# A graph network kernel: packed window lengths and running pair numbers kept in registers while the edge counts are made

## The chip, the cores and the metric

The program runs on one core of one Trainium2 chip. The metric is device time in microseconds (us) for one execution, lower is better. Before the change three executions took 4158.90, 4162.92 and 4170.17 us, so the median is 4162.92 us. All rows below come from one further execution that the hardware profiler took.

## The reference

Four graph layers run over N = 3125 nodes with 128 features and E = 100000 edges, given as `src` and `dst` with `dst` sorted. Each layer is followed by `x = layernorm(x + layer(x))`.

- Layer 0: an MLP over `concat(x[src], x[dst])` for each edge, two linear maps with batch norm and relu, summed over the edges of each `dst`.
- Layer 1: two graph convolutions with self loops and the norm `dinv[src] * dinv[dst]`, one along the edges and one against them.
- Layer 2: four steps `h = h + relu(tanh(A_norm @ (h @ Weff.T) - relu(h @ Asym.T)))`.
- Layer 3: attention with 8 heads over the edges, softmax over the edges of each target.

Layers 1 to 3, and the batch norm statistics of layer 0, need the edges only as a matrix of counts: `C[d, s]` is the number of edges from node s to node d. The kernel makes this matrix once and the change lies in that stage. `dst` is drawn as `3125 * u**2`, so low nodes have many edges and high nodes few.

## The kernel before, in words

Features are padded to NP = 3200 nodes. Every engine has its own program, and engines meet by semaphores only (`S[...]`). The stages are: preparation; the counts stage; degrees and batch norm statistics, which read the counts back; "pass 1" over the edges (layer 0, first map); "pass 2"; the graph convolutions; the four steps; attention.

The counts stage makes 100 windows (NWIN) of 32 targets each. The source axis is cut in four parts of 800, so a window is a 128 x 800 matrix in two PSUM banks: row 4*(target - 32*w) + (part of the source), column = source within its part. Edges come in pairs of 128-edge tiles: 392 pairs (NPAIR) of 256 edges. A window w visits the pairs `first` to `end - 1` that hold its targets, at least two. A pair on the border of two windows is visited by both. For each visit:

- VectorE (`one_hots`) builds for two tiles the one-hot rows of the sources (`one_src`, two 128 x 800 instructions, line 1392) and of the targets (`one_dst`, one 128 x 256 instruction, line 1394) in one of 8 slots (PAIRS). It waits for `slot_free` and tells `one_ready`.
- TensorE (`count_pair`) waits for `one_ready`, does four matmuls (two tiles, two halves of 400 columns, line 1746) into the banks `w mod 3` (SETS), and tells `slot_free`.

The slot and both semaphore values are worked out from a running number: `before + p` counts all visits so far from PAIR0 = 512 on, so `before` of a window is (visits done) - `first`. The function `window` (lines 388 to 397) gets these on each engine. It reads one packed word of the window from SBUF (`block_tab` row 3, `end * 512 + first`, line 390, a TENSOR_LOAD), takes it apart (lines 391 and 392), and either reads `before` from row 2 of the table (line 394, for the first window of a Python group) or works it out from the window ahead of it (line 396). Each value passes a range check, which is some register instructions and a SEQ_ASSERT.

TensorE's order in a window (`count_group`, lines 1767 to 1786; 12 windows are written out in a group and a hardware loop runs over the groups): `window`; wait until the low part of window w - 3 is out of the same banks (`lo_made`); the first pair; `low_part(w-2)`, which takes the bf16 part off what is in PSUM (line 1766); `source_degrees(w-3)` (line 1757); a hardware loop over the pairs that are left (line 1783); and a matmul with zeros that tells `window_done` (line 1785). VectorE's order (`count_four`, lines 1400 to 1408; four windows are written out): `window`, the first pair, and a hardware loop over the others (line 1407).

ScalarE (`evict`, `store_low`) handles each window in four passes: row counts and the bf16 part (lines 964 and 965), the f32 counts (line 966), the low part (line 976), a square that finds counts beyond bf16 (line 982). It issues three DMAs (lines 969, 970, 980). GpSimd gathers rows of `a_table` for pass 1 (line 817, 24 gathers in a round of six groups). It is told when it may go on: in the rounds 1 to 13 by `one_ready` at least 28 further visits on in each round, in the rounds 14 to 16 by `window_done`, at the last one 92 windows; after that it runs free. SP stores what was gathered (line 605). TensorE's fourth unit of pass 1 reads the first rows that GpSimd gathers straight into `a_direct`, after all 22 rounds.

The tables come from the preparation, on VectorE: `visits(block_tab, NWIN, PAIR0)` (line 1359) and one instruction that packs row 3 (line 1360). A helper on each engine, `do`, waits for each of these instructions before the next one.

Of the kernel before, what the change touches and what calls it, by code (L numbers as in the profile page):

```python
# [101 lines left out]
def gnn(nc, ins, out):  # L102
# [26 lines left out]
    with ctx:  # L129
# [54 lines left out]
        block_tab = sb("block_tab", [1, 4, NWIN], i32)  # L184
# [50 lines left out]
        lim_i = sb("lim_i", [NWIN, 2], i32)  # L235

# [94 lines left out]
        def bank(j, n=BANK):  # L331
            return psum[:, j * BANK:j * BANK + n]
# [55 lines left out]
        def window(eng, w, done_pairs):  # L388

            word = eng.value_load(block_tab[0:1, 3, ds(w, 1)], min_val=0, max_val=NPAIR * 512 + NPAIR)  # L390
            first = nc.s_assert_within(eng.snap(word & 511), 0, NPAIR - 2)
            end = nc.s_assert_within(eng.snap(word >> 9), 2, NPAIR)
            if done_pairs is None:
                before = eng.value_load(block_tab[0:1, 2, ds(w, 1)], min_val=PAIR0 - NPAIR, max_val=PAIR0 + NWIN * NPAIR)
            else:
                before = nc.s_assert_within(eng.snap((done_pairs - first) & 65535), PAIR0 - NPAIR, PAIR0 + NWIN * NPAIR)
            return first, end, before
# [858 lines left out]
        def _(dve):  # L1256
            v = nc.vector

            def do(i):
                stepped("dve", dve, i)  # L1260
# [98 lines left out]
            visits(block_tab, NWIN, PAIR0)  # L1359
            do(v.scalar_tensor_tensor(block_tab[:, 3, :], block_tab[:, 1, :], 512.0, block_tab[:, 0, :], ALU.mult, ALU.add))  # L1360
# [38 lines left out]

            def count_four(i):  # L1400
                done_pairs = None
                for q in range(4):
                    w = 4 * i + q
                    first, end, before = window(dve, w, done_pairs)
                    done_pairs = before + end
                    one_hots(w, first, before)
                    with dve.Fori(first + 1, end) as p:
                        one_hots(w, p, before)

# [310 lines left out]
        def _(pe):  # L1720
# [48 lines left out]

            def count_group(g, ms):  # L1770
                done_pairs = None
                for m in ms:
                    w = GROUP * g + m
                    known = isinstance(w, int)
                    first, end, before = window(pe, w, done_pairs)
                    done_pairs = before + end
                    after(pe, S["lo_made"], w + -2)
                    count_pair(m % SETS, first, before, True)
# [4 lines left out]
                    with pe.Fori(first + 1, end) as p:  # L1783
                        count_pair(m % SETS, p, before, False)
# [442 lines left out]
```

How the kernel before makes its waits and increments, by code:

```python
        def after(eng, s, n):  # L368
            if not (isinstance(n, int) and n <= 0):
                eng.wait_ge(s, n)
# [1 line left out]
        def hold(name, eng, s, n):  # L373
            eng.wait_ge(s, n)
            eng.sem_inc(held[name], 1)
# [42 lines left out]
        def stepped(name, eng, i):  # L419
            steps[name] += 1
            i.then_inc(step[name], 1)
            eng.wait_ge(step[name], steps[name])
# [13 lines left out]
        def stage_start(name, eng):  # L437
            passed[name] += 1
            for e in done:
                eng.wait_ge(done[e], passed[name])
# [47 lines left out]
        def root_act(act, to, of, bias):  # L489
            n = roots["act"] = roots["act"] + 1
            act.wait_ge(S["root_asked"], n)
            nc.scalar.activation(to, of, ACT.Sqrt, bias=bias).then_inc(S["root_made"], 1)
# [1 line left out]
        def root_dve(dve, to):  # L495
            n = roots["dve"] = roots["dve"] + 1
            dve.sem_inc(S["root_asked"], 1)
            dve.wait_ge(S["root_made"], n)
            stepped("dve", dve, nc.vector.reciprocal(to, to))
# [7 lines left out]
        def norm_pe(pe):  # L508
# [5 lines left out]
            def variances(c):  # L514
                pe.wait_ge(S["ln_sq"], squared + c + 1)
                for b in blocks_of(c):
                    last = nc.tensor.matmul(bank(7)[:, b:b + 1], z[:, b * P:(b + 1) * P], meanf[:, 0:1],
                                            start=True, stop=True)
                return last
# [7 lines left out]
            variances(NCH - 2)  # L527
            variances(NCH - 1).then_inc(S["ln_psum"], 1)
            pe.wait_ge(S["ln_dve"], given + 2 * NCH + 1)
            for c in range(NCH):
```

## Time and profile before

| what | value |
|---|---|
| median of three executions | 4162.92 us |
| profiled execution, its own time | 4158.93 us |
| its span, first to last instruction | 4157.3 us |
| TensorE busy in the span | 3405.6 us (82%) |
| VectorE busy | 2768.4 us (67%) |
| ScalarE busy | 1590.5 us (38%) |
| GpSimd busy | 1047.6 us (25%) |
| mean granted TensorE clock | 0.936 of full speed |

The profiled execution's own time is 1.6 us above its span and 4 us below the median. The counts stage runs from about 80 to 841 us, 18% of the span.
### The profile page before, as it was taken

To read this page: it belongs to the slowest core of one execution; us is meant where nothing else is said; L and a number is where in the kernel's file an instruction comes from. 1 tells how busy PE (TensorE), PEld (TensorE's weight loads), DVE (VectorE), ACT (ScalarE), POOL (GpSimd) and SP (SyncE) were. 2 spreads that over 40 slices of the span, in tenths; PEclk is the share of its full clock that TensorE was granted. 3 is DMA by queue.
4 is the path that set the end of the run, shared out by engine and by line. 5 is a ranking of instruction groups with operands and counts; after the bars stand their busy time and mean duration, and the time that the engine had idled before them with its cause. 6 is when DMAs were issued, how large, how long until landed. Compare 5 with 4: busy or idle time off the path is not lost. (4 is left out here: it accounts for less than half of the span.)

```text
span 4157.3 us, 85411 instructions
## 1 busy us (share of the span) xinstructions
PE 3405.6 (82%) x20244; PEld 1671.3 (40%) x20359; DVE 2768.4 (67%) x3753; ACT 1590.5 (38%) x2188; POOL 1047.6 (25%) x1132
## 2 busy tenths in 40 slices
PE   3777777777889967777989996699799989989996
PEld 1333333333444456666545554233322233332223
DVE  6887766623666655565122215799799989989995
ACT  2134455521222245543102111221198841118883
POOL 2877774566666312221000001000100000000000
PEclk8989899878999999999999998899899999999998
DMA  2245665667777667676646774411154431103343
GB/s 61 91 163 192 211 223 193 213 224 244 251 250 236 210 222 212 204 205 192 237 158 222 252 254 118 120 55 55 38 144 121 131 96 55 58 25 128 110 131 69
DMA packets 359411, 662.48 MB, mean 159 GB/s; under 512 B 134549, under 2 KB 221715, under 8 KB 358545
## 3 DMA queue, kind: packets, MB, share of 16 engines
q1 hardware_dynamic: 236288, 360.99, 27.4%
q10 hardware_dynamic: 97940, 248.84, 17.5%
q0 software_dynamic: 25088, 51.43, 4.7%
q8 instruction: 54, 0.88, 0.1%
q14 instruction: 41, 0.34, 0.0%
HBM read 428.22 MB, written 208.17 MB: 153 GB/s over the span
## 5 line engine op out<-in xcount | busy, mean ns | idle before, releaser
L817 POOL DMA_INDIRECT gat<-a_table,gidx x592 | 678.6, 1146 | 240.1 <-issue 138.4
L1697 DVE SCALAR_TENSOR_TENSOR pw<-ex,c_full 128x1564 f32<-128x1564 f32 x400 | 680.8, 1780 | 35.3 <-ACT ex L1235 30.7
L1235 ACT ACTIVATE ex<-psum 128x782 f32<-128x782 f32 x800 | 610.3, 826 | 77.2 <-PE psum L2117 61.0
L1659 DVE CUSTOM_DVE_ANT_0 masked<-psum,masks 128x1784 bf16<-128x1784 f32 x320 | 552.3, 1784 | 64.5 <-ACT masks L1208 43.4
L1746 PE MATMUL psum<-one_src,one_dst 128*128 x1968 | 420.2, 354 | 204.4 <-DVE one_dst L1394 117.4
L1392 DVE TENSOR_SCALAR one_src<-iota_sub,src_low 128x800 f16 x984 | 381.7, 429 | 196.8 <-PE psum L1746 115.0
L2126 PE MATMUL psum<-pw,vaug 128*32 128x391 f32 x3200 | 348.7, 508 | 29.8 <-DVE pw L1697 9.4
L1746 PEld LDWEIGHTS psum<-one_src,one_dst 128*128 x1968 | 189.7, 101 | 419.7 <-issue 336.0
L1208 ACT ACTIVATE masks<-masks,far 128x3128 bf16<-128x3128 bf16 x40 | 115.5, 2900 | 424.8 <-DMA masks<-ct_parts 424.8
L1058 ACT ACTIVATE r<-psum,vec 128x1024 f32<-128x1024 f32 x98 | 118.1, 1205 | 368.4 <-PE psum L1897 365.0
L1533 DVE SCALAR_TENSOR_TENSOR u<-psum,u 128x1024 f16<-128x1024 f32 x98 | 120.0, 1224 | 200.3 <-ACT u L1109 200.2
L1945 PE MATMUL psum<-w2s,r_in 128*128 128x128 f32 x1568 | 209.3, 289 | 35.8 <-issue 24.3
L1394 DVE SCALAR_TENSOR_TENSOR one_dst<-row_c,window_at,iota_row 128x256 f16 x492 | 233.9, 475 | 0.0
L2082 PE MATMUL psum<-qp,kp 96*128 96x446 bf16 (+1 forms) x700 | 173.0, 364 | 61.3 <-DVE mx L1659 31.8
L817 POOL DMA_INDIRECT a_direct<-a_table,gidx x192 | 184.3, 960 | 118.4 <-DMA a_direct<-a_table,gidx 58.7
L899 POOL TENSOR_TENSOR y<-y,visit_sum 128x128 f32 x122 | 102.3, 839 | 438.8 <-ACT visit_sum L1120 438.8
L1958 PE MATMUL psum<-u,ohd 128*128 128x128 f16 x1952 | 144.9, 226 | 82.8 <-issue 45.6
L1945 PEld LDWEIGHTS psum<-w2s,r_in 128*128 128x128 f32 x1568 | 191.2, 199 | 51.6 <-issue 43.8
L1499 DVE CAST dst_bc<-psum 128x1024 f16<-128x1024 f32 x98 | 120.0, 1225 | 114.7 <-PE psum L1897 109.8
L2087 PE MATMUL psum<-qp,kp 96*128 96x448 bf16 x800 | 189.6, 360 | 0.0
L1904 PE MATMUL psum<-r,W2T 128*128 128x512 f32 x392 | 184.3, 592 | 0.0
L2117 PE MATMUL psum<-kp,qp 99*128 (+1 forms) x800 | 173.0, 337 | 13.6 <-ACTq L1217 7.9
(350 smaller groups left out, 4842.9 us busy)
## 6 DMA issues: line engine op xcount, KB each, us to landing
c_full<-c_whole SPq DMA_DIRECT2D x80, 977.5 KB, 5.1
r_edges<-r ACTq DMA_DIRECT2D x98, 512.0 KB
r_in<-r_edges ACTq DMA_DIRECT2D x98, 512.0 KB, 3.9
c_ring<-ct_parts SPq DMA_DIRECT2D x100, 480.0 KB, 4.4
c_whole<-c_sum ACTq DMA_DIRECT2D x100, 400.0 KB
a_edges<-gat SPq DMA_DIRECT2D x148, 256.0 KB
a_in<-a_edges ACTq DMA_DIRECT2D x74, 512.0 KB, 4.3
c_ring<-ct_parts SPq DMA_DIRECT2D x100, 320.0 KB, 3.6
```

Source lines behind the costliest of these rows:

```text
L817: g.indirect_dma_start(to, None, a_table, bass.IndirectOffsetOnAxis(ap=gidx[:, s, k:k + 1], axis=0)).then_inc(landed, 16)
L1235: a.activation(ex[:, step_slot(n // 2), (n % 2) * 2 * CW:(n % 2 + 1) * 2 * CW].rearrange("p (h t) -> p h t", h=2), psum[:, o:o + 2 * BANK] ...
L1392: v.tensor_scalar(one_src[:, ds(slot, 1), t, 0:SUB].rearrange("p o n -> p (o n)"), iota_sub[:, :], src_low[:, ds(p * 2 + t, 1)], None, ALU ...
L1394: v.scalar_tensor_tensor(one_dst[:, ds(slot, 1), :, :].rearrange("p o t n -> p (o t) n"), row_c[:, ds(p * 2, 2)].rearrange("p (t o) -> p t ...
L1659: v.tensor_tensor_reduce(out=masked[:, n % 2, 0:count * width].rearrange("p (c t) -> p c t", c=count), in0=psum[:, first * BANK:(first + c ...
L1697: v.scalar_tensor_tensor(pw[:, step_slot(k), :].rearrange("p (h t) -> p h t", h=HQ), ex[:, step_slot(k), :].rearrange("p (h t) -> p h t", ...
L1746: last = t.matmul(bank(2 * k + half, n), one_dst[:, ds(slot, 1), s, :].rearrange("p o n -> p (o n)"), one_src[:, ds(slot, 1), s, half * HA ...
L1904: last = t.matmul(bank(4 + 2 * s + half), W["W2T"][:, :], r1[:, s, half * GE:(half + 1) * GE], start=True, stop=True)
L1945: last = t.matmul(psum[:, s * UE + k * P:s * UE + (k + 1) * P], r1_in[:, s, k * P:(k + 1) * P], w2s[:, :], start=False, stop=True, skip_gr ...
L2082: last = t.matmul(bank(first + c, width), kp[0:KQK, n // 2, ds(b * P, P)], query(quad, n // 2)[0:KQK, c0 + c * width:c0 + (c + 1) * width] ...
L2087: t.matmul(bank(7, 448), kp[0:KQK, n // 2, 0:P], query(quad, n // 2)[0:KQK, 0:448], start=True, stop=True)
L2126: last = t.matmul(psum[hh * HW:(hh + 1) * HW, 6 * BANK:6 * BANK + CW], vaug[:, k, quad * HQ + hh, :], pw[:, step_slot(k), hh * CW:(hh + 1) ...
```

## The change

TensorE no longer reads a word for each window. A new table `length_tab` has one word for three windows (SETS), with 9 bits for each window's number of pairs; TensorE reads it for each third window and takes the length by shift and mask. It no longer needs `first` (its slots and semaphore values need the running number only), so its loop runs over 1 to length - 1. The running number stays in a register, `pairs_taken`, that is copied into `before` with a range check and raised at the window's end. VectorE still needs `first`, to find the edges; it reads the packed words of four windows by one call ahead of the four windows, and keeps its own running number in a register. In the preparation, `visits(block_tab, ...)` (five instructions) goes, and six instructions that make `length_tab` come.

```diff
-        def window(eng, w, done_pairs):
-            word = eng.value_load(block_tab[0:1, 3, ds(w, 1)], min_val=0, max_val=NPAIR * 512 + NPAIR)
-            first = nc.s_assert_within(eng.snap(word & 511), 0, NPAIR - 2)
-            end = nc.s_assert_within(eng.snap(word >> 9), 2, NPAIR)
-            if done_pairs is None:
-                before = eng.value_load(block_tab[0:1, 2, ds(w, 1)], min_val=PAIR0 - NPAIR, max_val=PAIR0 + NWIN * NPAIR)
-            else:
-                before = nc.s_assert_within(eng.snap((done_pairs - first) & 65535), PAIR0 - NPAIR, PAIR0 + NWIN * NPAIR)
-            return first, end, before
+        def pairs_before(eng, total):
+            return nc.s_assert_within(eng.snap(total), PAIR0, PAIR0 + NWIN * NPAIR)
...
-            visits(block_tab, NWIN, PAIR0)
-            do(v.scalar_tensor_tensor(block_tab[:, 3, :], block_tab[:, 1, :], 512.0, block_tab[:, 0, :], ALU.mult, ALU.add))
+            do(v.scalar_tensor_tensor(block_tab[:, 2, :], block_tab[:, 1, :], 512.0, block_tab[:, 0, :], ALU.mult, ALU.add))
+            do(v.memset(lengths[:, :, :], 0))
+            do(v.tensor_tensor(lengths[:, :, :].rearrange("p t k -> p (t k)")[:, 0:NWIN], block_tab[:, 1, :],
+                               block_tab[:, 0, :], ALU.subtract))
+            for k in range(1, SETS):
+                do(v.tensor_single_scalar(shifted[:, :, k:k + 1], lengths[:, :, k:k + 1], 9 * k, op=ALU.logical_shift_left))
+            do(v.tensor_tensor(shifted[:, :, 0:1], lengths[:, :, 0:1], shifted[:, :, 1:2], ALU.bitwise_or))
+            do(v.tensor_tensor(length_tab[:, :].rearrange("p (t o) -> p t o", o=1), shifted[:, :, 0:1], shifted[:, :, 2:3],
+                               ALU.bitwise_or))
...
+            total_dve = dve.alloc_register("pairs_made")
+            dve.reg_mov(total_dve, PAIR0)
             def count_four(i):
-                done_pairs = None
+                words = nc.values_load_multi_w_load_instructions(
+                    block_tab[0:1, 2, ds(4 * i, 4)], engines=[dve.engine], min_val=0, max_val=NPAIR * 512 + NPAIR)[1]
                 for q in range(4):
+                    first = nc.s_assert_within(dve.snap(words[q] & 511), 0, NPAIR - 2)
+                    end = nc.s_assert_within(dve.snap(words[q] >> 9), 2, NPAIR)
+                    before = nc.s_assert_within(dve.snap((pairs_before(dve, total_dve) - first) & 65535), PAIR0 - NPAIR,
+                                                PAIR0 + NWIN * NPAIR)
                     w = 4 * i + q
-                    first, end, before = window(dve, w, done_pairs)
-                    done_pairs = before + end
                     one_hots(w, first, before)
                     with dve.Fori(first + 1, end) as p:
                         one_hots(w, p, before)
+                    dve.reg_add(total_dve, total_dve, end - first)
...
+            total_pe = pe.alloc_register("pairs_taken")
+            pe.reg_mov(total_pe, PAIR0)
             def count_group(g, ms):
-                done_pairs = None
                 for m in ms:
...
-                    first, end, before = window(pe, w, done_pairs)
-                    done_pairs = before + end
+                    if m % SETS == 0:
+                        word = pe.value_load(length_tab[0:1, ds((GROUP // SETS) * g + m // SETS, 1)], min_val=0,
+                                             max_val=NPAIR << 9 * (SETS - 1) | NPAIR << 9 | NPAIR)
+                    length = nc.s_assert_within(pe.snap((word >> 9 * (m % SETS)) & 511), 2, NPAIR)
+                    before = pairs_before(pe, total_pe)
                     after(pe, S["lo_made"], w + -2)
-                    count_pair(m % SETS, first, before, True)
+                    count_pair(m % SETS, 0, before, True)
...
-                    with pe.Fori(first + 1, end) as p:
+                    with pe.Fori(1, length) as p:
                         count_pair(m % SETS, p, before, False)
+                    pe.reg_add(total_pe, total_pe, length)
```

## Rows read from the trace of the kernel before

**Rows 1.** Two stretches: us, busy (x) PE, PEld, DVE, ACT, POOL; clock, DMA, GB/s.

```profile
79.00:554.00 475.00, 348.62 (x1646) 156.95 (x1647) 373.91 (x1007) 165.27 (x290) 382.57 (x353) 0.91 0.48 161
554.00:842.00 288.00, 208.95 (x1012) 92.39 (x1010) 177.00 (x471) 166.82 (x300) 164.46 (x190) 0.90 0.61 209
```

**Rows 2.** Who waited for whom, 80 to 851: total us, times, longest.

```profile
PEld psum L1746 <- issue: 336.0, 455, 4.1
DVE one_src L1392 <- PE psum L1746: 115.0, 86, 2.4
DVE one_src L1392 <- issue: 80.8, 54, 2.6
POOL gidx L814 <- PE psum L1785: 66.3, 13, 20.9
```

**Rows 3.** Waits for a pair (whole stage, then before 554.5 us); windows closed.

```profile
L1746 PEldq ALU_OP  x492: 32/36/36, 83.5 to 839.1; - x164
...
L1746 PEldq ALU_OP  x330: 32/36/36, 83.5 to 553.1; - x165
...
L1785 PE MATMUL psum<-zerosb x100: 167/167/172, 130.7 to 841.0; 128*128 128x1 bf16 x100
```

**Rows 4.** Timeline: stage's start, seven pairs of the 41-pair window: start, us, what.

```profile
79.62 0.82 PE L1739 MATMUL psum<-zerosb 128*4 128x400 bf16 x2 [3.10 <-POOLq L434]
...
90.93 0.75 DVE L1392 TENSOR_SCALAR one_src<-iota_sub,src_low 128x800 f16 x2
91.81 0.85 PE L1746 MATMUL psum<-one_src,one_dst 128*128 x4 [0.28 <-issue]
...
97.35 0.76 DVE L1392 TENSOR_SCALAR one_src<-iota_sub,src_low 128x800 f16 x2
98.78 0.85 PE L1746 MATMUL psum<-one_src,one_dst 128*128 x4 [0.32 <-DVE one_dst L1394]
```

**Rows 5.** Register instructions: duration min/median/max ns, first and last start.

```profile
L390 PEldq TENSOR_LOAD <-block_tab x100: 297/314/1034, 79.7 to 835.8; - x100
L391 PEldq ALU_OP  x200: 36/37/42, 80.6 to 836.5; - x100
L392 PEldq FUSED_REGOPS  x100: 194/196/207, 80.8 to 836.7; - x100
L396 PEldq FUSED_REGOPS  x182: 57/102/151, 132.0 to 837.2; - x182
L1783 PEldq FUSED_REGOPS  x492: 47/47/88, 84.3 to 839.0; - x164
L390 DVEq TENSOR_LOAD <-block_tab x100: 301/314/936, 79.9 to 822.6; - x100
```

**Rows 6.** The same for one window, 708.4 to 714.8 us.

```profile
L390 PEldq FUSED_REGOPS  x2: 46/102/157, 708.5 to 709.0; - x2
L396 PEldq SEQ_ASSERT  x1: 18/18/18, 710.4 to 710.4; - x1
```

**Rows 7.** Timeline of ScalarE at two windows.

```profile
704.64 0.15 ACT L964 ACTIVATE row_counts<-psum 128x1 f32 x1
...
709.80 0.15 ACT L964 ACTIVATE row_counts<-psum 128x1 f32 x1
```

**Rows 8.** Timeline: long gathers of GpSimd, and VectorE's idle time at one's end.

```profile
87.87 50.01 POOL L817 DMA_INDIRECT gat<-a_table,gidx  x1 [0.30 <-DMA gat<-a_table,gidx]
...
169.30 5.07 POOL L817 DMA_INDIRECT gat<-a_table,gidx  x1 [0.30 <-DMA gat<-a_table,gidx]
...
174.52 0.77 DVE L1392 TENSOR_SCALAR one_src<-iota_sub,src_low 128x800 f16 x2 [0.96 <-PE psum L1746]
```

**Rows 9.** TensorE's line 1880 in pass 1, 980 to 1040: a direct unit; idle before.

```profile
L1880 PEld LDWEIGHTS psum<-identb,a_direct x32: 95/102/147, 1009.9 to 1030.1; 128*128 128x128 f16 x32
...
  DMA a_direct<-a_table,gidx: 9.6, 2
```

**Rows 10.** Timeline: one small VectorE instruction of the preparation.

```profile
78.13 0.17 DVE L1377 TENSOR_SCALAR scale_up<-expo 128x3 int32<-128x3 int32 x1
```

More of the change, by code:

```diff
@@ L183, in gnn @@
         unit_tab = sb("unit_tab", [1, 4, NU], i32)
-        block_tab = sb("block_tab", [1, 4, NWIN], i32)
+        block_tab = sb("block_tab", [1, 3, NWIN], i32)
+        length_tab = sb("length_tab", [1, -(-NWIN // SETS)], i32)
         parts_tab = sb("parts_tab", [1, 8], i32)
@@ L235, in gnn @@
         lim_i = sb("lim_i", [NWIN, 2], i32)
+        lengths = sb("lengths", [1, -(-NWIN // SETS), SETS], i32)
+        shifted = sb("shifted", [1, -(-NWIN // SETS), SETS], i32)
         at[0] = after_gather
```

## The prediction, made before the kernel was run

> **What bounds the kernel now.** I read the stretches of the counts stage first [rows 1]. In both, no engine is full: TensorE is busy 349 of 475 us and 209 of 288, VectorE 374 and 177, ScalarE 165 and 167, GpSimd 383 and 164. So something that a busy share doesn't count must set the pace. The waits [rows 2] show it: TensorE's weight loads stand idle 336 us in 455 places for "issue", that is for nothing but their own sequencer, while VectorE waits 115 us for TensorE. The next view is the long first window, where nothing but pairs goes on [rows 4]. TensorE starts its pairs at 91.81 to 98.78, six steps of (98.78 - 91.81) / 6 = 1.162 us, while VectorE makes them at (97.35 - 90.93) / 6 = 1.07 us. A pair is on TensorE for 0.85 us only, so 1.162 is what its sequencer takes for one pass of the loop.
>
> Now the sum over the stage. There are 492 pairs, 330 of them before 554 us, and 100 windows [rows 3]. Windows 0 to 49 are those before 554 (the page of the stretch ends where the 51st begins). The stage runs from 79.62 [rows 4] to 841.2 [rows 3], 761.6 us. The pairs take 492 x 1.162 = 571.7, which leaves 189.9, or **1.90 us for a window**. By halves: (474.4 - 330 x 1.162) / 50 = 1.82 and (287.2 - 162 x 1.162) / 50 = 1.98. Two parts of the stage with quite another mix of pairs and windows give the same cost, so TensorE's sequencer bounds both. One window shows what the 1.9 us are [rows 6]: its register work starts at 708.5 and the last range check starts at 710.4, so with the instructions of the semaphore wait behind it there are 2.0 us in which TensorE gets nothing.
>
> **What the change takes from TensorE's sequencer.** The 2.0 us hold 13 instructions, whose durations are 0.367 for the load here (0.314 in the median) and 0.02 to 0.20 for the others [rows 5], 1.15 in sum. The start to start distances add the rest: (1.95 - 1.15) / 13, so 0.06 us behind each.
> - Gone in each window: the check of `first` (0.27), the check of `end` (0.33, with the 0.196 instruction), `before` (0.49, with two register instructions, an ALU instruction and the check), and the `first + 1` of the loop (0.047 + 0.06 = 0.11). That is 1.20 us.
> - Gone in 66 of 100 windows: address, load, its range check and assert, 0.046 + 0.367 + 0.157 + 0.018 and 4 x 0.06, so 0.83 us.
> - New in each: shift, mask and check of the length, no row shows it, taken as between the 0.33 of `end` and the 0.49 of `before`, 0.40; the checked copy of the register, as `end`, 0.33; the addition, 0.10. That is 0.83 us.
> So a window without a load gives 1.20 + 0.83 - 0.83 = 1.20 us, one with a load 0.37. Over 66 and 34 windows this is 92 us, 0.9 a window. The bounds: with each new check at the dearest row (0.49 twice) 0.65 a window; with checks that cost an ALU instruction (0.1) only, and the loads at the stretched durations that rows 5 have up to 1.03, 1.3. I take 0.95. The loop over the pairs keeps its instructions, and the first pair, the low part and the degrees keep their order.
>
> The profiler's account of these instructions is partial: the Trainium skill (Perfetto Trace Analysis, Per-engine timelines) says that for an instruction of the sequencer only its execution is shown, not its decode and semaphore push. The trace agrees, 1.15 us of durations in 1.95 us. By durations alone the saving would be near 0.55 a window.
>
> **What VectorE gains.** It keeps `first` and `end` of each window, reads four words in one call (probably four loads of 0.31 to 0.94 [rows 5] with four checks, no row shows them together), and gets one more check (0.33) and two additions. What leaves is one load of `before` in four windows and the load from the window's own preamble. I put this at no net change: it stands 1.5 us at a window now (80.8 / 54 in rows 2), 1.1 at best and 2.3 if each load in the call takes 0.94.
>
> **What is late next.** With TensorE at 1.162 a pair and 0.95 a window, the halves are:
> - Windows 0 to 49: TensorE 330 x 1.162 + 50 x (1.82 - 0.95) = 427 us. VectorE 330 x 1.07 + 50 x 1.5 = 428 us. They tie; with 8 slots between them both lose a little at the borders, 432. Saved: 474 - 432 = 42 us.
> - Windows 50 to 99: TensorE 162 x 1.162 + 50 x 1.03 = 240 us, VectorE 173 + 75 = 248 us. But ScalarE has a fixed cycle for a window, whatever its pairs: from one eviction to the next at 709.80 - 704.64 = 5.16 us without a wait for TensorE at either end [rows 7]. 50 x 5.16 = 258 us. Saved: 287 - 258 = 29 us.
> So the stage ends some 71 us earlier, of which I keep 68 for the handovers from one bound to the next.
>
> **GpSimd** then has to be asked. It waits 66.3 us in 13 places for windows to close [rows 2], all after 630 us, so its gathers can move up by about 66 us and no more. TensorE's pass 1 depends on them: its first direct unit starts at 1009.9 and TensorE stood 9.6 us for those gathers [rows 9], so the end of the gathers sets the start of pass 1. What ends last is GpSimd's shift, 66 less what it loses when the three DMAs of ScalarE come closer together. I take 64 us in all. Behind pass 1 nothing reads the counts stage, so the shift stays whole.
>
> The preparation gets six small instructions for five, one more at 0.17 us and its wait [rows 10], 0.3 us; it is within the rounding.
>
> **The sum.** 4158.9 (the profiled execution's own time) - 64 = 4095. That execution lies 4 us below the median of the three, so I forecast **4099 us** for the median.
>
> **Rivals.**
> - *GpSimd starves or falls behind*, 4122 us. For it: one gather lasted 50.01 us while VectorE ran without a gap, another 5.07 us and ended (174.37) inside VectorE's next gap (173.56 to 174.52) [rows 8]. A VectorE with fewer and shorter gaps lets fewer gathers through. If one gather in each second window of the first 50 waits 1 us more, GpSimd loses 25 us and only 40 of its slack are left: 4163 - 41. Against it: VectorE still stops at each window for about 1.5 us. The Trainium skill (SBUF — State Buffer, on the shared port pair and the "DVE blocks DMA" trap) says that a VectorE instruction in a two-port mode locks GpSimd out of writing descriptors. The gather of 50 us agrees; by that rule too the loss depends on the gaps that are left.
> - *VectorE becomes the bound*, 4144 us. If its call for four words takes the long loads, it stands 2.1 us a window: 330 x 1.07 + 50 x 2.1 = 458 and 173 + 105 = 278, so it saves 16 + 9 = 25 less handovers, some 19 us. For it: VectorE's loads reach 0.936 [rows 5]. Against it: the median is 0.314.
> - *Slower*, 4190 us. If the running register costs the loop more register instructions in each pass (it can't be folded as the old sum was), each costs 0.11 us in 392 passes (492 - 100), 43 us. Two of them eat the 90 us that the preambles give; it decides from there, and three give 4163 + 129 - 92 = 4200, less what VectorE's slack absorbs. Against it: the old `before` was a register as well.
> - *The checks are dear*, 4109 us: 0.65 a window in place of 0.95 makes the first half 383.5 + 50 x 1.17 = 442 us in place of 432, and leaves the second to ScalarE.
>
> **Chances.** The forecast, 4084 to 4112 with the dear checks in it: 0.68. GpSimd: 0.15. VectorE: 0.07. Below 4084 (ScalarE's cycle shrinks too, or GpSimd keeps ahead): 0.06. Slower or nothing: 0.04. The range for 8 in 10 is 4082 to 4126. Differences below 0.3%, 12.5 us, can't be told from no change. Faster by more than that: 0.94; within: 0.03; slower: 0.03.
>
> **What would show each step.** The pace in the long window stays 1.16 us on TensorE (if it is longer, the slower rival has come). TensorE's loads of the window table drop from 100 (line 390) to 34, with about 0.9 us of register work in a window without one. The last zero matmul of line 1785 comes at 773 us. From window 50 on, the evictions of line 964 come each 5.2 us, and TensorE or VectorE waits for ScalarE. VectorE's wait of 115 us for TensorE shrinks to half or less. GpSimd's 66 us of waits for line 1785 fall under 20, and the first direct unit of pass 1 starts near 946. A stage that ends 68 us earlier with a pass 1 that starts less than 55 us earlier would prove the GpSimd rival; a VectorE that stands over 2 us at each window, the VectorE rival. All of it is wrong if the stage ends less than 40 us earlier.

## The result and the profile after

| | before | after |
|---|---|---|
| median on the same chip | 4166.55 us (4 runs) | **4117.26 us** (4 runs, 4108.64 to 4123.13) |
| ratio to before | 1 | **0.9879**, interval 0.9856 to 0.9902 |
| profiled execution, its own time | 4158.93 us | 4115.29 us |
| its span | 4157.3 us | 4113.6 us |
| mean granted TensorE clock | 0.936 | 0.947 |

The change takes about 49 us off by the medians, 44 by the two profiled executions. Medians here and below leave out two executions that stand far outside all others (8201.58 us once in e5, 4447.88 us once in e9). The forecast was 4099 (range 4082 to 4126): the direction, the stage and the range were right, and 18 us of the expected gain did not come.

The stretches of the counts stage in the kernel after, the first up to the 50th zero matmul, the second up to the last (columns as in [rows 1]):

```profile
80.00:514.00 434.00, 328.22 (x1654) 151.42 (x1654) 370.80 (x1010) 166.08 (x293) 358.45 (x291) 0.97 0.48 162
514.00:774.00 260.00, 187.57 (x1000) 87.19 (x1000) 175.35 (x467) 164.81 (x298) 201.20 (x230) 0.97 0.72 249
```

VectorE is now busy 371 of 434 us, 85%, in the first stretch. In the second no busy share tells the bound (TensorE 188 of 260, VectorE 175, ScalarE 165, GpSimd 201); ScalarE's own rows below do. The zero matmuls and the register rows of TensorE and VectorE in the kernel after (duration min/median/max in ns, first and last start), against [rows 3, 5]:

```profile
L1801 PE MATMUL psum<-zerosb x100: 163/164/168, 131.7 to 772.9; 128*128 128x1 bf16 x100
L1788 PEldq TENSOR_LOAD <-length_tab x34: 297/331/1024, 79.3 to 765.7; - x34
L393 PEldq FUSED_REGOPS  x100: 181/181/187, 80.5 to 766.7; - x100
L1407 DVEq TENSOR_LOAD <-block_tab x25: 352/357/960, 79.4 to 739.8; - x25
```

The last zero matmul starts at 772.9 in place of 841.0. TensorE has 34 loads in place of 100. VectorE's call for four words is **one** load of 0.357 us, not four. The pace of the loop, in the long first window (start, duration, engine and line; two starts with four passes between them left out):

```profile
92.28 0.85 PE L1756 MATMUL psum<-one_src,one_dst 128*128 x4 [0.23 <-issue]
...
98.14 0.85 PE L1756 MATMUL psum<-one_src,one_dst 128*128 x4 [0.33 <-DVE one_dst L1397]
```

That is (98.14 - 92.28) / 5 = 1.17 us against 1.16 in [rows 4]: the change costs the loop nothing. The waits of the kernel after (us in total, times, longest), against [rows 2]:

```profile
PEld psum L1756 <- issue: 295.2, 432, 5.0
PE psum L1756 <- DVE one_dst L1397: 93.3, 108, 4.3
DVE one_src L1395 <- PE psum L1756: 74.2, 61, 3.3
DVE one_src L1395 <- issue: 55.3, 59, 3.6
PE psum L1756 <- ACT c_lo L972: 44.1, 27, 2.9
```

VectorE's waits for TensorE fell from 115.0 to 74.2 us, and TensorE now stands 44.1 us for ScalarE's pass over the low part. GpSimd has next to no wait for a window's close left (1.2 us), where [rows 2] had 66.3 us. ScalarE's row counts late in the stage come 5.21 and 5.14 us apart and wait for nobody, as in [rows 7]:

```profile
702.58 0.15 ACT L960 ACTIVATE row_counts<-psum 128x1 f32 x1
707.79 0.15 ACT L960 ACTIVATE row_counts<-psum 128x1 f32 x1
712.93 0.15 ACT L960 ACTIVATE row_counts<-psum 128x1 f32 x1
```

Then pass 1, where the missing time is. Its units through DRAM (`a_in`), its direct units, and GpSimd's gathers for these:

```profile
L1896 PE MATMUL psum<-identb,a_in x1184: 218/219/314, 918.2 to 1423.7; 128*128 128x128 bf16 x198
L1896 PE MATMUL psum<-identb,a_direct x384: 216/219/315, 969.7 to 1414.3; 128*128 128x128 bf16 x192
L813 POOL DMA_INDIRECT a_direct<-a_table,gidx x192: 938/944/1191, 958.3 to 1368.8; - x192
```

The same three rows of the kernel before:

```profile
L1880 PE MATMUL psum<-identb,a_in x1184: 219/219/314, 986.6 to 1465.7; 128*128 128x128 bf16 x198
L1880 PE MATMUL psum<-identb,a_direct x384: 216/219/311, 1009.9 to 1456.3; 128*128 128x128 bf16 x192
L817 POOL DMA_INDIRECT a_direct<-a_table,gidx x192: 938/944/1227, 995.8 to 1411.3; - x192
```

TensorE begins pass 1 68.4 us earlier (986.6 to 918.2), the whole of the stage's gain. GpSimd comes to its direct gathers only 37.5 us earlier (995.8 to 958.3). The last unit of pass 1 starts 42.0 us earlier, so 26 us are lost inside it. Behind that, nothing changed: 4158.93 - 1465.7 = 2693.2 and 4115.29 - 1423.7 = 2691.6 us.

Where GpSimd lost its time, two gathers of the kernel after and what VectorE did as the second began:

```profile
87.21 56.45 POOL L813 DMA_INDIRECT gat<-a_table,gidx  x1 [0.30 <-DMA gat<-a_table,gidx]
188.54 25.37 POOL L813 DMA_INDIRECT gat<-a_table,gidx  x1 [0.30 <-issue]
```
```profile
188.38 0.75 DVE L1395 TENSOR_SCALAR one_src<-iota_sub,src_low 128x800 f16 x2
189.06 0.47 DVE L1397 SCALAR_TENSOR_TENSOR one_dst<-row_c,window_at,iota_row 128x256 f16 x1
189.46 0.75 DVE L1395 TENSOR_SCALAR one_src<-iota_sub,src_low 128x800 f16 x2
...
212.62 0.47 DVE L1397 SCALAR_TENSOR_TENSOR one_dst<-row_c,window_at,iota_row 128x256 f16 x1
213.35 0.76 DVE L1395 TENSOR_SCALAR one_src<-iota_sub,src_low 128x800 f16 x2 [0.26 <-issue]
```

VectorE shows no gap from 188.5 on until the one of 0.26 us ahead of 213.35, and the gather that was issued at 188.54 ends at 213.91. Most gathers take about 1 us. Before, the one long gather was 50.01 us [rows 8]; the two of after are 81.8 together. All 528 gathers ahead of the direct ones, from 80 us to the first direct gather, are these (us, GpSimd's time in them, clock, DMA share, GB/s), the kernel before first:

```profile
80.00:995.80 915.80, 617.50 (x528) 0.89 0.55 190
```
```profile
80.00:958.30 878.30, 641.54 (x528) 0.93 0.59 201
```

So the gathers grew by 24.0 us: the long ones by 31.8, while the others shrank by 7.8. The time between gathers fell from 298.3 to 236.8 us, by 61.5: the 66.3 us of waits are gone, and 4.8 us of others came. That gives 61.5 - 24.0 = 37.5 us, the shift that was measured.

### The profile page after: what moved, and what is told of

It is laid out like the page before. It is cut to its first block and busy times, and to the rows that moved or that the text cites. A ratio compares the mean times of both kernels' runs of the same rounds, so it can differ in the third digit from the quotient of the medians.

```text
span 4113.6 us, 85171 instructions
## 1 busy us (share of the span) xinstructions
PE 3380.3 (82%) x20358; PEld 1658.0 (40%) x20359; DVE 2761.8 (67%) x3754; ACT 1587.9 (39%) x2188; POOL 1075.1 (26%) x1132
## 3 DMA queue, kind: packets, MB, share of 16 engines
q1 hardware_dynamic: 236288, 360.99, 27.6%
## 5 line engine op out<-in xcount | busy, mean ns | idle before, releaser
L813 POOL DMA_INDIRECT gat<-a_table,gidx x592 | 703.3, 1188 | 245.6 <-issue 151.7
L1756 PE MATMUL psum<-one_src,one_dst 128*128 x1968 | 401.6, 340 | 177.8 <-DVE one_dst L1397 93.3
L1395 DVE TENSOR_SCALAR one_src<-iota_sub,src_low 128x800 f16 x984 | 380.3, 427 | 130.0 <-PE psum L1756 74.2
L2098 PE MATMUL psum<-qp,kp 96*128 96x446 bf16 (+1 forms) x700 | 171.7, 362 | 61.5 <-DVE mx L1669 31.6
```

What stands on the lines that cost most here:

```text
L813: g.indirect_dma_start(to, None, a_table, bass.IndirectOffsetOnAxis(ap=gidx[:, s, k:k + 1], axis=0)).then_inc(landed, 16)
L1395: v.tensor_scalar(one_src[:, ds(slot, 1), t, 0:SUB].rearrange("p o n -> p (o n)"), iota_sub[:, :], src_low[:, ds(p * 2 + t, 1)], None, ALU ...
L1756: last = t.matmul(bank(2 * k + half, n), one_dst[:, ds(slot, 1), s, :].rearrange("p o n -> p (o n)"), one_src[:, ds(slot, 1), s, half * HA ...
L2098: last = t.matmul(bank(first + c, width), kp[0:KQK, n // 2, ds(b * P, P)], query(quad, n // 2)[0:KQK, c0 + c * width:c0 + (c + 1) * width] ...
```

## The experiments

Each was timed beside the kernel before on the same chip (medians of it 4164.6 to 4169.2), but not all on one chip, so runs are compared by their ratios to the kernel before, or by their traces.

**The two halves of the change, each alone.** My theory was that TensorE's sequencer bounds the stage and the gain is all on that side; the rival, that VectorE's shorter stops give some of it.

```diff
 # e3_pe_only: TensorE as after, VectorE as before; both tables made
+                done_pairs = None
                 for q in range(4):
+                    first, end, before = window(dve, w, done_pairs)
+                    done_pairs = before + end
 # e4_dve_only: VectorE as after, TensorE as before
+                    first, end, before = window(pe, w, done_pairs)
+                    done_pairs = before + end
...
-                    with pe.Fori(1, length) as p:
+                    with pe.Fori(first + 1, end) as p:
```

> Only TensorE's half of the change: TensorE loads one packed length word for three windows and keeps the running number, VectorE keeps its word for each window as before (both tables are made, six instructions more in the preparation, about 1 us). If TensorE's sequencer bounded the stage alone, nearly all of the 68 us come: stage end at 773 to 785 us. Theory G: VectorE's load at each window leaves it gaps, so no gather takes over 10 us but the one in the first window, and the kernel takes 4100 to 4115 us, no slower than the whole change. Rival T: 4117 to 4125 us, slower than the whole change, as VectorE's half of the gain is missing.

> Only VectorE's half: four words in one call and a running register on VectorE, TensorE as before the change. If TensorE's sequencer is the bound, the stage ends at 836 to 841 us as before and the time is 4157 to 4170 us, ratio 0.998 to 1.001. If VectorE's windows were part of the bound (the ring of 8 handing its stops on to TensorE), the stage ends 10 us or more earlier.

TensorE's half: 4120.77 us, ratio 0.991 (0.9891 to 0.9928). VectorE's half: 4170.12, ratio 1.0014 (1.0006 to 1.0023). The zero matmuls of each, e3 first, then e4:

```profile
L1806 PE MATMUL psum<-zerosb x100: 163/164/211, 132.3 to 771.8; 128*128 128x1 bf16 x100
```
```profile
L1807 PE MATMUL psum<-zerosb x100: 167/167/172, 132.8 to 839.2; 128*128 128x1 bf16 x100
```

The whole stage gain is TensorE's: 771.8 against 772.9 with both halves. VectorE's half gives the stage 1.8 us and the kernel no gain. Of the expectation for e3, the stage's end and the gathers came true (none of over 10 us but the first, 57.51). The time did not: I had 4100 to 4115 us, and it came where the rival had it, though the rival's reason, a part of the stage's gain missing, is refuted. The single stall of 25.37 us is thus not what counts. In e3 it is absent, yet the 528 gathers take 643.9 us in sum, as long as after.

**The packing of three lengths in a word.** The change with one length word for each window, all else kept:

```diff
-                    if m % SETS == 0:
-                        word = pe.value_load(length_tab[0:1, ds((GROUP // SETS) * g + m // SETS, 1)], ...)
+                    word = pe.value_load(length_tab[0:1, ds(w, 1)], min_val=0, max_val=NPAIR)
...
```

> The changed kernel, but TensorE reads a length word for each window (no packing of three); the running number stays in the register. This adds 66 loads with their checks, 0.83 us each by my account. Windows 0 to 49: 33 x 0.83 = 27 us later if TensorE is their bound alone, less if VectorE ties; windows 50 to 99: TensorE at 240 + 27 = 267 in place of ScalarE's 260, 7 us later. So the stage ends 25 to 34 us later than 773, and the time is 4130 to 4150 us. If packing is worth nothing (a load hides behind the matmuls in the queue), the stage ends at 773 to 780.

4130.04 us, ratio 0.9905 (0.9891 to 0.992).

```profile
L1792 PE MATMUL psum<-zerosb x100: 163/163/168, 131.1 to 787.9; 128*128 128x1 bf16 x100
```

The stage is 15.0 us longer than after (787.9 against 772.9), 12.2 of it in the first 50 windows. The time is at the low end of what I expected, but the stage is a miss: I had it 25 to 34 us longer. So 66 loads are worth 15 us beside the other bounds, and 53 of the 68 come without them, by the rest of the register work that went. The prediction priced a load and its check at 0.83 us, 33 of them in the first half at 27 us, and 12.2 came. That VectorE, nearly as slow as TensorE there, takes over is the likely reason; no run shows it by itself.

**Does VectorE's gapless run hold GpSimd up?** The prediction's rival says so. The edit lets VectorE run at most 4 visits ahead of TensorE in windows 0 to 11, in place of 8, so that it must pause. The stage is bound by TensorE there, and should lose little. e2 is the same edit on the kernel before, as a control: GpSimd had 66 us of waits for windows there.

```diff
-                dve.wait_ge(S["slot_free"], before + p + 1)
+                dve.wait_ge(S["slot_free"], before + p + (1 + PAIRS - depth))   # depth 4 for windows 0 to 11
```

> The changed kernel, but in windows 0 to 11 VectorE may be at most 4 visits ahead of TensorE and not 8, so it stops a little at each visit. Theory G (GpSimd's gathers starve while VectorE runs without a gap, and their end sets the start of pass 1): the gathers of 56 and 25 us go, GpSimd is some 70 us ahead and waits for windows again, the first direct unit of pass 1 comes near 930 in place of 970 us, and the kernel takes 4085 to 4095 us, ratio 0.980 to 0.983 to the kernel before. Rival T (the missing 15 us lie in the counts stage or in pass 1 itself): the time stays at 4117 us, ratio 0.988. Both expect the stage to end at 773, or some us later if VectorE's lead was needed in these windows.

> The kernel before with the same limit of 4 visits in windows 0 to 11. Theory G: no change, 4160 to 4172 us, ratio 0.998 to 1.002, since GpSimd had 66 us of slack: the gather of 50 us goes, and GpSimd's waits for windows rise from 66 to about 115 us. Rival T has no use for GpSimd and expects the same time. A gain of more than 10 us would say that the starved gathers cost time before the change too, and that my account of the slack is wrong.

e1: 4102.66 us, ratio 0.9855 (0.984 to 0.9869), 15 us faster than the change alone by the medians and 10 by the ratios, whose intervals overlap a little. e2: 4166.07, ratio 1.0 (0.9989 to 1.0012). The longest gather of e1, and its direct units:

```profile
88.21 20.02 POOL L813 DMA_INDIRECT gat<-a_table,gidx  x1 [0.31 <-DMA gat<-a_table,gidx]
```
```profile
L1897 PE MATMUL psum<-identb,a_direct x384: 216/219/314, 944.1 to 1395.1; 128*128 128x128 bf16 x192
```

The stalls of 56.45 and 25.37 us became one of 20.02, and no other gather in the stage takes over 4.01. The 528 gathers take 597.8 us in sum, 43.7 less than after. The stage itself ends 3.7 us later than after (776.6), yet the direct units start 25.6 us earlier and pass 1 ends 19.1 us earlier (1404.6 against 1423.7). So 10 to 15 of the missing 18 us are back. It is less than I expected (4085 to 4095 us, first direct unit near 930, where it came at 944.1), since GpSimd ran into the windows' closes again and waited 27.1 us for them. e2 has the time that I expected, but GpSimd's waits for windows rose to 81.7 us only, not to 115.

So the stalls did make GpSimd late. What ends a stall can be read from the traces too. In e1 it ended at 108.23, and VectorE's rows there are:

```profile
106.25 0.76 DVE L1395 TENSOR_SCALAR one_src<-iota_sub,src_low 128x800 f16 x2
107.32 0.76 DVE L1395 TENSOR_SCALAR one_src<-iota_sub,src_low 128x800 f16 x2
108.43 0.77 DVE L1395 TENSOR_SCALAR one_src<-iota_sub,src_low 128x800 f16 x2
109.61 0.77 DVE L1395 TENSOR_SCALAR one_src<-iota_sub,src_low 128x800 f16 x2
```

VectorE's step from visit to visit was 1.07 us from the stall's start on and became 1.11 and then 1.18 us, TensorE's pace: it had reached its limit, though no idle time is shown. Over all 14 traces, 147 gathers that began before 700 us took more than 2.5 us. Of these, 132 ended 0.89 to 0.98 us behind the first moment at which VectorE started a one-hot instruction more than 15 ns later than back to back, and 13 of the others 0.14 to 0.19 us ahead of it. So a stalled gather stands until VectorE lets up, and then takes its usual time. What starts a stall stays open. A VectorE without a gap is not enough, for in the kernel after the three gathers ahead of the stall of 25.37 us passed in 1.10, 1.14 and 1.03 us under the same gapless run. The last two:

```profile
185.64 1.14 POOL L813 DMA_INDIRECT gat<-a_table,gidx  x1 [0.30 <-DMA gat<-a_table,gidx]
187.20 1.03 POOL L813 DMA_INDIRECT gat<-a_table,gidx  x1 [0.16 <-issue]
```

The rule of the Trainium skill behind the prediction's rival (SBUF — State Buffer, SBUF: two separate sides, the "DVE blocks DMA" trap) agrees in kind. The same page (A bandwidth-pool intuition that's wrong) gives a number for one VectorE instruction, a transfer blocked until its end and about 115 ns more. Here a gather stood through whole chains of instructions, up to 56.45 us. What happens on the port itself no run here isolates.

**GpSimd not held by windows.** With e1's limit, GpSimd also no longer waits for `window_done` in rounds 14 to 16 (e5); e10 is the same on the kernel before.

```diff
             with pool.Fori(11, 14) as i:
-                gather(i + 3, S["window_done"], 9 * i + -33, (0, 2, 3, 5, 6, 8))
+                gather(i + 3)
```

> The limit of 4 visits in windows 0 to 11, and GpSimd is no longer held for closed windows in its rounds 14 to 16. Theory G: in the kernel with the limit alone GpSimd was held until 735 us and the first direct unit came at 944, with 6 us of TensorE's wait; without the holds the gathers move up by 15 to 20 us, that wait goes, and the time falls by about 6 us to 4093 to 4099 us, ratio about 0.984. Rival C (the holds spare the counts stage from DMA contention): the stage ends later than 777 us by more than GpSimd gives, and the time is 4103 us or more.

> The kernel before the change with the limit of 4 visits in windows 0 to 11 and with the free GpSimd. If the start of pass 1 was bound by the counts stage there (first unit at 986.6, first direct unit 9 us late), only this lateness can go: 4150 to 4162 us, ratio 0.996 to 0.999, and the changed kernel with both edits keeps a lead of 70 us or more over it. If the two edits are worth the 35 us by themselves that they gave the changed kernel, the time is 4135 us or less.

e5: 4079.67 us, ratio 0.9786 (0.9772 to 0.98), 13 us under the expected range. Its first direct gather comes 12.1 us earlier than in e1 and its pass 1 ends 15.6 us earlier; the first direct unit waits for no gather now. Where the rest of the step from e1 comes from is open. e10: 4145.9, ratio 0.9951 (0.9938 to 0.9964), 4 us under its range. Its rows are the clearest of the study, as GpSimd is far ahead there, 114 us earlier than before:

```profile
L1881 PE MATMUL psum<-identb,a_in x1184: 219/219/314, 986.6 to 1449.0; 128*128 128x128 bf16 x198
L817 POOL DMA_INDIRECT a_direct<-a_table,gidx x192: 938/944/4092, 881.7 to 1373.7; - x192
```

Pass 1 starts at 986.6 as before, but takes 462.4 us in place of 479.1. So the kernel before already lost 17 us in pass 1 to late gathers. It stood only 9.6 us ahead of the first direct unit [rows 9]; the rest were small waits in later units.

**Other work of the stage.** Each of these is e5 with one more edit. e6 leaves out ScalarE's square, and so the finding of counts beyond bf16 (zero stands for it). e8 and e9 leave out range checks of TensorE: e8 both that of the length and that of the running number, e9 the second alone.

```diff
 # e6_no_square
-                after(act, S["over_ready"], w)
-                a.activation(over_out[:, :], c_lo[:, q, :], ACT.Square, accum_out=over[:, ds(w, 1)]
-                             ).then_inc(S["over_ready"], 1)
+                act.sem_inc(S["over_ready"], 1)
...
-            do(v.tensor_reduce(out=over1[:, :], in_=over[:, :], op=ALU.max, axis=AX.X))
+            do(v.memset(over1[:, :], 0.0))
 # e9_one_check (e8 does the same to length)
-                    before = pairs_before(pe, total_pe)
+                    before = nc.s_assert_within(pe.snap(total_pe), PAIR0, PAIR0 + NWIN * NPAIR,
+                                                skip_runtime_bounds_check_because="...")
```

> The kernel with the limit and the free GpSimd, without ScalarE's square over the low part (the finding of counts beyond bf16 is left out, and zero is put in its place). If ScalarE's cycle of 5.2 us bounds windows 50 to 99, they take 4.7 to 4.8 us each (TensorE's and VectorE's sums of 240 and 248 us for 50), so the stage ends 15 to 22 us earlier, and the time is 4075 to 4085 us if GpSimd follows, or 4090 if GpSimd's gathers are the end again. If ScalarE was no bound, the stage ends at 777 as before and nothing moves.

> The kernel with the limit and the free GpSimd, and TensorE without the range checks of the length and of the running number, which takes some 0.5 us of register work from each of its windows. My account has TensorE and VectorE tie in windows 0 to 49 (427 and 428 us) and ScalarE bound the rest, so the stage should end only 0 to 8 us earlier and the time stay within 6 us of the kernel with the checks. If TensorE's sequencer is still the bound alone, windows 0 to 49 end 25 us earlier.

> The kernel with the limit and the free GpSimd, and TensorE without the range check of the running number alone, so that its loop over the pairs keeps the same eight instructions; 0.3 us of register work less in each window. If TensorE and VectorE tie in windows 0 to 49 and ScalarE bounds the rest, windows 0 to 49 end 0 to 5 us earlier than the 384 us they take with the check (last zero matmul of the 50th less the first), and the rest stays at 5.2 us a window; the time stays at 4078 to 4085 us. If TensorE's sequencer alone bounds the first half, it ends 15 us earlier.

e6: 4094.46 us, ratio 0.9817 (0.9801 to 0.9833), **slower** than e5 (0.9786) with 20.6 us less of stage: the stage came as expected, the time did not. e8: 4083.16, ratio 0.9801 (0.9784 to 0.9818). e9: 4081.24, ratio 0.9798 (0.9782 to 0.9814). The last two can't be told from e5. The zero matmuls of e6 and, below, its row counts late in the stage:

```profile
L1800 PE MATMUL psum<-zerosb x100: 163/164/168, 130.9 to 753.1; 128*128 128x1 bf16 x100
...
701.94 0.17 ACT L960 ACTIVATE row_counts<-psum 128x1 f32 x1 [0.92 <-ACT c_lo L972]
706.51 0.17 ACT L960 ACTIVATE row_counts<-psum 128x1 f32 x1 [0.98 <-PE psum L1800]
```

ScalarE was the bound of the last 50 windows. Without the square they take 4.80 us each in place of 5.17 in e5 (5.20 after), ScalarE's row counts wait for TensorE, and TensorE's waits for ScalarE's low part fall from 43.2 to 3.5 us. But GpSimd's first direct gather came 6.7 us later than in e5 (921.8 against 915.1), so TensorE started pass 1 at 897.4, then waited 21.2 us ahead of the first direct unit, and pass 1 took 500 us. GpSimd's gathers were 4.9 us shorter in sum than in e5, and the time between them 11.7 us longer; what made it so is open.

In e8 the loop got slower. Register instructions of TensorE's sequencer on the line of the loop over the pairs, e8 and then e5:

```profile
L1801 PEldq FUSED_REGOPS  x634: 47/47/68, 85.4 to 771.3; - x159
L1801 PEldq ALU_OP  x542: 32/36/36, 86.4 to 772.1; - x181
```
```profile
L1799 PEldq FUSED_REGOPS  x392: 47/47/52, 84.7 to 771.7; - x196
L1799 PEldq ALU_OP  x392: 36/36/36, 85.6 to 772.4; - x196
```

That is 242 + 150 = 392 more, one for each pass, and in the long first window a pass takes 1.265 us in the mean in place of 1.158, +0.11. So a value without its check seems not to be kept, but worked out again in each pass. The saved preambles paid for it (the last zero matmul stands at 773.2, in e5 at 773.7), so that the expectation for e8 met the time by luck.

e8 also tells on GpSimd, with an edit of TensorE alone. Its slower loop holds VectorE back from the first window on: the longest gather is 11.5 us, the 528 gathers take 590.4 us in place of 611.8 in e5, and with the stage's end unchanged the first direct gather comes 27.6 us earlier.

e9 keeps the length's check, and its loop is at 1.169. Its stage ends 11 us earlier (762.7), 9.8 of them in windows 0 to 49. I had expected 0 to 5 if TensorE and VectorE tie and 15 if TensorE's sequencer bounds them alone, so the truth lies between the two: two thirds of what is taken from the sequencer still come through there.

**The limit at 3 visits**, on e5 (e11) and on e9 (e12):

```diff
             for i in range(3):
-                count_four(i, 4)
+                count_four(i, 3)
```

> The changed kernel with free GpSimd and a limit of 3 visits in place of 4 in windows 0 to 11, as the candidate for the fastest version. If the first gather of 22 us was waiting for VectorE's first stop, which comes after about a dozen visits less with each visit of lead taken away, it falls to 5 to 12 us, GpSimd reaches pass 1 some 10 us earlier, and pass 1 is up to 8 us shorter: 4070 to 4080 us. If 3 visits are too few to cover TensorE's borders between windows, the stage ends over 5 us later than 774 and the gain is lost: 4082 to 4092 us.

> The same without TensorE's range check of the running number. With the limit of 4 this made the counts stage 12 us shorter and the time no shorter, since GpSimd was late for pass 1 (TensorE waited 13 us for the first direct unit). If GpSimd is 10 us further with the limit of 3, half of the 12 us come through: 4066 to 4076 us. If GpSimd still arrives late, the time is that of the kernel with the check within 5 us.

e11: 4080.23 us, ratio 0.9794 (0.9781 to 0.9807): the stage ends 9 us later (782.6), the longest gather of the stage is 5.1 us and GpSimd is 32 us earlier (882.8); the two cancel. e12: **4070.89 us, ratio 0.9775 (0.9762 to 0.9788)**, as expected. It is 94 us under the kernel before on its chip, 9 us under e11 on the same chip, and by the two ratios 1.0% better than the change alone. Its ratio is the lowest of all, but its interval overlaps those of e5 and e9.

```profile
L1803 PE MATMUL psum<-zerosb x100: 163/163/211, 132.2 to 767.2; 128*128 128x1 bf16 x100
...
L1898 PE MATMUL psum<-identb,a_in x1184: 219/219/314, 912.3 to 1372.3; 128*128 128x128 bf16 x198
L813 POOL DMA_INDIRECT a_direct<-a_table,gidx x192: 938/944/1172, 891.5 to 1311.2; - x192
```

**One rule over all runs.** Times are starts in us; the last column is the later of (first direct gather + 471) and (first `a_in` unit + 460). I chose the two constants to fit these runs, so the rule sums them up and was not tested on others.

| run | last zero matmul | first `a_in` unit | first direct gather | last `a_in` unit | by the rule |
|---|---|---|---|---|---|
| before | 841.0 | 986.6 | 995.8 | 1465.7 | 1467 |
| after | 772.9 | 918.2 | 958.3 | 1423.7 | 1429 |
| e1 | 776.6 | 923.2 | 927.2 | 1404.6 | 1398 |
| e2 | 842.1 | 986.4 | 1002.0 | 1474.1 | 1473 |
| e3 | 771.8 | 918.4 | 954.8 | 1424.0 | 1426 |
| e4 | 839.2 | 984.0 | 997.5 | 1466.0 | 1469 |
| e5 | 773.7 | 918.8 | 915.1 | 1389.0 | 1386 |
| e6 | 753.1 | 897.4 | 921.8 | 1397.5 | 1393 |
| e7 | 787.9 | 933.7 | 964.9 | 1435.7 | 1436 |
| e8 | 773.2 | 919.5 | 887.5 | 1378.4 | 1380 |
| e9 | 762.7 | 908.5 | 921.9 | 1396.0 | 1393 |
| e10 | 840.4 | 986.6 | 881.7 | 1449.0 | 1447 |
| e11 | 782.6 | 928.1 | 882.8 | 1390.2 | 1388 |
| e12 | 767.2 | 912.3 | 891.5 | 1372.3 | 1372 |

Two bounds meet in pass 1. If GpSimd's direct gathers start less than some 11 us ahead of TensorE's pass 1, GpSimd sets its end, otherwise TensorE's own 460 us do. In the kernels before and after it is GpSimd, and in e6 and e9 too, which is why their shorter stages brought nothing (TensorE waited 21.2 and 13.5 us ahead of the first direct unit). The rule is within 7 us in each row.

## Why the prediction was right or wrong

- **TensorE's sequencer bounds the stage: right.** The sum by halves said 42 + 29 less 3 for handovers, 68 us. The runs gave 42.5 + 25.6 = 68.1, and e3 shows that TensorE's half alone makes it.
- **The pace of the loop stays: right** (1.17 us). The slower rival's mechanism is real, though. e8 met it, at the price put on it: 0.11 us a pass, which is 43 us over 392 passes. It had come into e8 by the loss of a check, not by the register.
- **The saving of 0.95 us a window: nearly right.** It can't be read off the stage, since other engines bound it now, but TensorE's sequencer shows it. From the first register instruction of a window to the end of its last range check it took 2.02 us in the mean before (the 77 windows that have all 13 instructions of [rows 6]). After, it takes 0.88 in the 66 windows without a load and 1.76 in 33 with one. With 0.05 more at the loop's start that saves 1.19 and 0.31 us, where the prediction had 1.20 and 0.37; over 66 and 34 windows it is 0.89 a window. How much of a part comes through in the stage is another matter: 12.2 / 33 = 0.37 us for a load and its check (e7) and 9.8 / 50 = 0.2 for a check (e9), where the prediction priced the work at 0.83 and 0.33.
- **VectorE, no net change: right** (e4). That the call would be four loads was wrong; it is one of 0.357 us.
- **What is late next: right in the second half, half right in the first.** ScalarE's cycle holds windows 50 to 99 at 5.20 us (5.16 forecast), and e6 shows it by taking work off ScalarE. In windows 0 to 49 VectorE is nearly full, but e9 shows that TensorE's sequencer still sets much of the pace, so the tie that was worked out isn't a whole one. VectorE's waits for TensorE fell to 74.2 us, not to half of 115.
- **GpSimd: wrong, and this is the error.** The prediction took "66 less what it loses when the three DMAs of ScalarE come closer together", and kept 64. The term that it lost to was another: the 24.0 us by which the gathers grew, 31.8 in the stalls less 7.8 in the rest. The shift was 37.5. The rival named it and gave 4122 us, 5 from the median. Its 25 us of loss are close to the 24.0 by some luck, as it had 1 us in each second window where two long stalls came. The argument against it ("VectorE still stops at each window for about 1.5 us") used the mean of the windows that show a stop. It left out VectorE's other stops, those for TensorE, which the prediction itself had shrink to half. The kernel before has such a stop at 190.2 us, 1.74 us long (row below), where the kernel after has none from 188.5 to 213. A TensorE that loses less at each window lets VectorE run on. e3 fits this: it has VectorE's old code, and its first direct gather (954.8) and pass 1 (505.6 us) are as late and as long as after. e8 shows the other side, a slower TensorE and shorter gathers.

```profile
191.97 0.85 DVE L1392 TENSOR_SCALAR one_src<-iota_sub,src_low 128x800 f16 x2 [1.74 <-PE psum L1746]
```

- **The sign that was to tell the two apart** worked, but was worded loosely. "Pass 1 starts" had to mean its first direct unit: this came 40.2 us earlier, at 969.7 and not near 946, and under the bound of 55, while its first unit of all came 68.4 earlier.
- **"Pass 1 depends on them by its start": too narrow.** Late gathers also lengthen the rest of it, 505.5 us against a floor of about 460. That the kernel before lost 17 us there was in its trace and not seen, and the expectation for e10 missed by the same step.

What happens on the port stays open, as does what starts a stall: the runs varied VectorE's pauses, not the form of its instructions. That the first stall is still 20 us with a limit of 4 follows from the rows of e1: VectorE first fills its lead without a pause, and the stall ends as it meets the limit. With a limit of 3 its steps grow from 88.2 us on, and the longest stall is 5.1.

## What to carry to other kernels

Divide a stage's time by its two counts, here passes and windows, in two parts with another mix: if one pair of costs fits both, a sequencer may be the bound, and its register work has a price that busy shares hide. Then price it from the sequencer's own rows, start to start, for durations alone show about half of it. Before you count on an idle engine's slack, ask what a faster neighbour does to it: a VectorE without pauses held up GpSimd's gathers, and a lower limit on VectorE's lead, where it was ahead anyway, gave back 10 to 15 us. And when a stage gets shorter, find out which of the engines that feed the next one arrives last; only what moves that one counts.

## What the runs showed of the hardware

- A load of four neighbouring words into four registers was one TENSOR_LOAD of 0.357 us in the median on VectorE, against 0.31 for one word before [rows 5].
- A gather of GpSimd that takes about 1 us otherwise (0.97 in the median after) stood for up to 56.45 us while VectorE ran back to back, and the one of 25.37 us ended 0.6 us behind a gap of only 0.26 us. In 14 traces, 132 of the 147 gathers of over 2.5 us ended 0.89 to 0.98 us behind VectorE's first late start. Other gathers passed in 1.03 to 1.14 us under the same gapless run.
- Leaving out a range check can make a loop slower: one register instruction more in each pass, +0.11 us (e8).
- On TensorE's sequencer a window's 13 instructions ahead of its first pair's wait take 2.02 us in the mean, though their durations sum to about 1.15 us in the window that the prediction read.
- The mean granted clock in the stage was 0.97, where it was 0.91 and 0.90 before [rows 1], so it was at the upper of its two levels (2.4 GHz) for more of the time. TensorE's busy share hardly moved: 349/475 = 73% and 209/288 = 73% before, 328/434 = 76% and 188/260 = 72% after. What raised it was not tried, and no run sets apart what it gave. An estimate for the first half: at the lower level (1.2 GHz) pairs start 1.34 us apart (first window of the kernel before, 85.1 to 89.1 us), at the upper 1.16. By the mean clocks the lower level held for 2 x 0.09 x 475 = 86 us before and 2 x 0.03 x 434 = 26 after. The 60 us less are worth at most some 60 x (1 - 1.16 / 1.34) = 8 of the 42 us.
